# Row-maximum chunks that end at seven ninths of a unit, and a shift transpose five slots behind them, in a multi-query attention kernel

## What is computed

```python
q = (x @ Wq).reshape(b, s, 32, 32); k, v = split(x @ Wkv)
scores = einsum('bqhd,bkd->bhqk', q, k) * scale
scores = where(causal, scores + slopes[:, None, None] * (kpos - qpos), -inf)
attn = softmax(scores)
out = einsum('bhqk,bkd->bqhd', attn, v).reshape(b, s, 1024) @ Wo
x = layernorm(x + out)
```

## Time and profile before

| | |
|---|---|
| median of 3 runs | 4188.78 us |
| lowest and highest run | 4184.06, 4193.92 us |
| profiled execution: its own time | 4190.77 us |
| its span from the first to the last instruction | 4189.0 us |
| TensorE, share of the span busy | 91% |
| VectorE | 59% |
| ScalarE | 46% |
| GpSimd | 32% |
| mean granted TensorE clock, as a share of 2.4 GHz | 0.953 |

### The profile page before, as it was taken

How to read it: one execution, slowest core, us unless ns; L and a number is a source line. 1 busy time by engine, 2 the same in 40 slices (tenths; PEclk the granted TensorE clock), 3 DMA queues, 4 the chain that set the end, 5 groups by cost and what they waited for, 6 DMA issues and landing times. The chain is left out here.

```text
span 4189.0 us, 73921 instructions
## 1 busy us (share of the span) xinstructions
PE 3813.9 (91%) x22065; PEld 2365.4 (56%) x22065; DVE 2476.4 (59%) x4462; ACT 1927.4 (46%) x3253; POOL 1359.9 (32%) x420
## 2 busy tenths in 40 slices
PE   5989989999999997798999999999999599999998
PEld 3555554445444443555555444544444288888887
DVE  4556666666766672455776667766665244444444
ACT  2436555565666565344664656566566400000000
POOL 1114434444444454111443444445454200000010
PEclk8889999999999998878999999999999899999999
DMA  2111110000000001111111000000000311111111
GB/s 72 39 49 33 30 41 24 20 22 22 14 19 14 19 6 34 54 42 44 32 28 41 22 22 22 14 19 14 19 14 6 131 56 60 60 60 60 60 60 51
DMA packets 159069, 152.11 MB, mean 36 GB/s; under 512 B 8388, under 2 KB 141508, under 8 KB 156584
## 3 DMA queue, kind: packets, MB, share of 16 engines
q1 hardware_dynamic: 158696, 147.70, 11.9%
HBM read 96.75 MB, written 33.62 MB: 31 GB/s over the span
## 5 line engine op out<-in xcount | busy, mean ns | idle before, releaser
L509 ACT ACTIVATE prob<-ps_s,alibi 128x512 f32<-128x512 f32 (+3 forms) x2560 | 1522.6, 623 | 1206.5 <-PE ps_s L771 613.3
L589 DVE TENSOR_REDUCE mxp<-ps_a 128x1 f32<-128x512 f32 (+3 forms) x2560 | 1460.1, 605 | 864.2 <-PE ps_a L710 445.2
L452 POOL TENSOR_TENSOR prob<-prob 128x2048 f32<-128x2048 f32 (+1 forms) x240 | 1043.7, 4349 | 1209.4 <-ACT prob L509 1209.3
L771 PE MATMUL ps_s<-qst,kexp 97*128 97x512 f32 (+3 forms) x2560 | 1103.1, 442 | 133.8 <-ACT prob L509 96.1
L707 PE MATMUL ps_a<-kmax,qst 97*128 97x512 f32 (+3 forms) x2560 | 962.1, 402 | 32.6 <-DVE mxp L589 14.9
L771 PEld LDWEIGHTS ps_s<-qst,kexp 97*128 97x128 f32 x2560 | 498.0, 196 | 814.8 <-ACT prob L509 531.6
L794 PE MATMUL ps_o<-prob,val 128*32 128x512 f32 (+3 forms) x5120 | 617.2, 555 | 7.5 <-ACT prob L509 7.5
L707 PEld LDWEIGHTS ps_a<-kmax,qst 97*128 97x128 f32 x2560 | 505.3, 199 | 111.2 <-DVE mxp L589 56.6
L794 PE MATMUL ps_sum<-prob,ones 128*32 128x512 f32 (+3 forms) x3200 | 363.3, 527 | 0.0
L980 POOL TENSOR_TENSOR hb_sb<-h_sb,bias_b 128x1024 f32<-128x1024 f32 x32 | 76.8, 2401 | 791.4 <-DVE z_sb L1124 732.3
L607 DVE RECIPROCAL r_sb<-s_sb 128x128 f32<-128x128 f32 x256 | 233.8, 931 | 123.8 <-ACT s_sb L515 121.6
(11 more groups left out here) (148 smaller groups left out, 3710.6 us busy)
## 6 DMA issues: line engine op xcount, KB each, us to landing
wq_raw<-in_L_attn_Wq SPq DMA_DIRECT2D x65, 512.0 KB, 3.7
xs<-in_L_attn_hidden_states SPq DMA_DIRECT2D x9, 2048.0 KB, 8.2
qst<-qst SPq DMA_DIRECT2D x64, 256.0 KB
att_scratch<-at_sb SPq DMA_DIRECT2D x64, 256.0 KB, 2.3
at_raw<-att_scratch SPq DMA_DIRECT2D x32, 512.0 KB, 5.4
x_sb<-in_L_attn_hidden_states SPq DMA_DIRECT2D x32, 512.0 KB, 4.3
out<-z_sb SPq DMA_DIRECT2D x32, 512.0 KB, 3.2
z_sb<-in_L_attn_Wo SPq DMA_DIRECT2D x4, 512.0 KB, 5.6
```

The costliest lines, as they stand in the source:

```text
L452: nc.gpsimd.tensor_tensor(even[:, :, c1:], even[:, :, c1:], odd[:, :, c1:], ALU.add).then_inc(pair_done, 1)
L509: nc.scalar.activation(prob[slot][:, h, c0:], ps_s[bank][:, c0:], ACT.Exp, bias=alibi_of(u, h, k - QT * s)).then_inc(e_done, 1)
L589: nc.vector.tensor_reduce(mxp[:, h * QT + t, c:c + 1], ps_a[bank][:, 0:cols], AX.X, ALU.max).then_inc(a_done, 1)
L771: last = nc.tensor.matmul(ps_s[bank][:, c0:], kexp[0:KR, k * P:(k + 1) * P], qst[buf][0:KR, h, c0:], start=True, stop=not diagonal)
```

## The change

Two numbers of the plan change, both for segments 1 to 3 alone.

```diff
-    a_slots = slots - (7 if s else 6)
+    a_slots = slots * 7 // 9 if s else slots - 6
...
-        at.setdefault(a_slots + 2, []).append(("CT", 0))
+        at.setdefault(a_slots + (5 if s else 2), []).append(("CT", 0))
```

## The result

| | before | changed |
|---|---|---|
| median | 4186.69 us (4 runs) | 4245.24 us (4 runs) |
| lowest and highest run | 4184.06, 4193.92 | 4235.15, 4251.44 |
| profiled execution: its own time | 4190.77 | 4235.15 |
| its span | 4189.0 | 4233.3 |
| mean granted TensorE clock | 0.953 | 0.954 |

The ratio of the medians is 1.0135 (95% interval 1.0109 to 1.016): the change makes the kernel slower by some 58 us. The forecast was 4194 us, with a range up to 4210. The profiled execution of the changed kernel is the fastest of its four, so a comparison of the two traces has 44 us to explain, not 58.

What follows compares the result with a forecast made beforehand. TensorE, busy for 91% of the span, was taken as the bound. The terms -6.0 - 10.4 - 4.1 + 13.4 + 11.9 = +4.8 us on the profiled 4190.8 gave 4195.6, as median 4194 us; range 4176 to 4210.

Steps and rivals of the forecast that it cites:

- Rival B: Slower: VectorE becomes the bound of the first seven ninths, plus two half-clock stretches; together +16, 4210 us; chance 0.25.
- Part 1: TensorE's wait in the shift's transpose: removing it gives 0.25 us in 24 loop units of segments 2 and 3, -6.0 us.
- The DMA still lands in time: Segment 1's later transpose: 3.3 us remain for 0.7 us of transpose and copy and 1.8 us to landing.
- Part 2: Chunks leaving the unit's end: -10.4 us in segment 3's loop units, -4.1 us in segment 2's.
- Rival D: Ends without chunks fall to half clock: 24 units pay some 3 us, +72 us, 4266 us; chance 0.01.
- part 3: Chunks squeezed into the first seven ninths of loop units: +13.4 us in segment 3, +11.9 us in segment 2.
- part 4: Units written out: unit 6 of segments 1 and 2 gains about 3 us, segment 2's unit 7 loses +1.5 per batch; together 0.

Runs made afterwards that it cites:

- ct_only: The kernel before with chunks unchanged and, in segments 1 to 3, the transpose four slots behind them instead of two: 4192.92 us, ratio 1.0026.
- chunks_only: The kernel before with only the chunks of segments 1 to 3 ending earlier (seven ninths), the transpose still two slots behind: 4283.98 us, ratio 1.0243.

## Why the prediction was wrong

The forecast was "no change" at 4194; it came out 51 us higher, outside the range. Rival B named the direction and one of the two mechanisms, at 4210, and its price was too low.

**What held.** Part 1: the wait in L715 was to fall from 63.9 to about 25; it is 25.0. That such a wait is worth much less than its length at the full clock is what ct_only shows; the forecast took -0.25 us a unit, and alone the step gains nothing, -0.42 in step 14 against +0.29 and +0.4 behind it. The shift's operation takes 0.17 to 0.18 us in the loop units of segment 2 and 2.97 to 3.18 in those of segments 1 and 3, where an addition of GpSimd runs beside it. That is what the Trainium skill (SBUF — State Buffer, on the two physically separate sides) made of it, by its rule of the exclusive lock: free in segment 2, held in 1 and 3; the trace agrees, and five slots cover either.

One sentence of part 1 did not hold: "The DMA still lands in time", whose failure in segment 1 was to show it "wrong altogether". The first S behind five of segment 1's transposes waits for it, 0.5 to 1.2 us each and 4.3 in all, and before none did. Behind the three loop units among them the DMA took 2.8 to 3.3 us to land; where it took the usual 1.8 it was there 0.8 us ahead. It is a small part of the loss.

Part 2: the last four steps of a segment 3 unit were to lose 0.87 + 0.25 = 1.12 us and lose 1.11 (5.11, 3.66, 4.27, 3.69 to 4.62, 3.41, 3.72, 3.87). In segment 2 the forecast was -0.34 - 0.25 = -0.59 us, and the last steps show -0.56. Steps 12 and 13, priced by a step with chunks against the same step without them, came out within 0.02 us. Steps 14 and 15 were right in their sum alone: -0.55 and +0.18, where -0.39 and 0 had been forecast.

Rival D fell as given: in the changed kernel's loop units the ends without chunks keep the full clock; the lower clock came in its fullest steps and in unit 6, each time behind waits.

**The step that failed first: part 3,** "the chunks that are squeezed into the first seven ninths", taken at +1.12 us a unit in segment 3 and +0.99 in segment 2; measured +2.26 and +1.60.

- "Steps 4, 5, 8 and 9 get theirs in the second half, where TensorE sat idle for 0.27 us ... enough for one interval of 0.23: 0." Right for 8 and 9 (4.69 and 3.66). Steps 4 and 5 grew by 0.37 and 0.54. The idle time that I read in step 9 stands in a step without query copies; steps 4 and 5 carry two copies and a reciprocal on VectorE, which was busy for 4.66 of 5.20 us there. Halved reductions take 0.52 of 5.20 off step 4 and 0.29 of 5.00 off step 5.
- "I take 0.23 unmasked": step 3 grew by 0.24, but step 7 by 0.43. There the first S stands 1.67 us ahead of PV (1217.54 to 1219.21), not 1.24 plus 0.23, and the intervals between its matmuls are wider, as this timeline of TensorE shows:

```profile
1217.54 0.50 PE L771 MATMUL ps_s<-qst,kexp 97*128 97x512 f32 x1
1217.88 0.39 PE L707 MATMUL ps_a<-kmax,qst 97*128 97x512 f32 x1
1218.23 0.50 PE L771 MATMUL ps_s<-qst,kexp 97*128 97x512 f32 x1
1218.57 0.71 PE L707 MATMUL ps_a<-kmax,qst 97*128 97x512 f32 x2
1219.21 1.06 PE L794 MATMUL ps_o<-prob,val 128*32 128x512 f32 x8
```

  From S to the chunk it is 0.34 us here, against 0.23 in the earlier trace rows, which I had taken as a chunk's interval everywhere.
- Segment 2: "step 7 -0.30" measured -0.05, "step 5 +0.23" measured +0.51, "steps 3 and 4 +0.3" beside the chunks' own +0.23, 0.53 in all, measured +0.62.
- The rest of segment 3: steps 0 and 1 +0.37 (forecast +0.46), step 11 +0.40 (+0.30), steps 6 and 10 -0.04 (-0.2).
- The lower clock: Rival B counted two such stretches in the whole kernel. There is one in 7 of 12 loop units of segment 3 and in 2 of 12 of segment 2, at 1.3 to 1.4 us each, some 12 us. Two waits of 0.60 and 0.24 us in one step are followed by the lower clock in some units and not in others.

**The step that failed second: part 4,** "together 0", with unit 6 gaining about 3 us. Unit 6 of segment 2 costs +12.1 us and unit 7 +7.9 in the trace. I had followed the chunks and the transpose through the order, and not the other items whose place depends on `a_slots`. "The change adds and removes no instruction" was true, but the clip to `a_slots - 1` moves two copies and the weights' split in unit 6 of segment 2 as well, and three copies and the split by one slot in that of segment 1. No rival named it.

The account nearly closes on the 64 us of segments 1 to 3: the forecast's own 4.8, 13.7 and 7.3 more in part 3's steps (1.14 and 0.61 in 12 units each), 12 for the lower clock in the loops, 21.9 in the units written out, and 2.4 in segment 1's loop make 62.

In Rival B's own terms: its mechanism (VectorE's queue in the packed head) cost not 16 us but some 34 in the 24 loop units, clock included: 39.9 - 6.3, what halved reductions take away. The jam in unit 6, the second mechanism, came on top.

## What to carry to other kernels

When a number that spreads work is changed, list every item of the plan whose place is computed from it, clips and `min` included, and look at the fullest unit, not the typical one. The price of work squeezed into a stretch is read from the step in which the engine that must digest it is fullest (here VectorE at 90%), and two short waits that meet in one step can be followed by a half-clock stretch that costs more than they do (1.3 us behind 0.84). If chunks must be denser somewhere, their slot inside the step matters as much as their number: behind the PV they cost next to nothing where VectorE has room (steps 8 and 9), ahead of it 0.24 to 0.43 us each.

## What the runs showed that I had not expected

- TensorE's granted clock falls behind quite short waits when they come together: behind a 0.60 and a 0.24 us wait in one step the next 4 us stand at 0.57; behind a 1.16 us wait the next 8 stand at 0.57; around a wait of 1.99 us in unit 6, 16 us stand at 0.60. In the first case the next step is back at its length within 0.1 us; in the last the rest of the unit runs slow in one batch, and the rest but for the last step in the other. By the Trainium skill (TensorE: Matmul & The Clock Gate, "What's actually happening") the full clock is granted to activity and half is the default state; the windows above agree in that each fall stands behind idle time of TensorE, busy for 3.12 of the 4 us ahead of the first one. The price is 1.3 us in the mildest case and some 6 in the worst.
- The same program text gets this in some turns and not in others: step 5 of the first unit of a turn in segment 3 takes 5.00 us once and 6.3 three times. The third unit has it in every turn and the second in none, though their plans are the same.
- The interval of one more chunk is not a constant: 0.23 us in a run without waits, 0.34 where the S had to wait for an exponential with its weight load too (1217.54 to 1217.88; the weight load of that S stood idle for 0.48 us until then).
- A transpose that waits in TensorE's queue for VectorE costs 0 to 0.25 us at the full clock, and with a half-clock stretch behind it 2.9 us (6.95 instead of 4.05 in chunks_only's step 7).
